# Residuals as identity matmuls in PSUM, norms that read the banks, and ScalarE as writer of the normalized values

## The reference, cut to what matters

```
x = layernorm(x + attention(x))         # attention: projections, conv, state recurrence, gate, @ Wo.T
x_q = where(x > .33, .5, where(x < -.33, -.5, 0))
x = layernorm(x + x_q @ w_rram.T)       # layernorm: (x - mean) / sqrt(var + 1e-5)
```

## Time and profile before

| | us |
|---|---|
| median of 3 runs | 454.32 (451.31 to 454.52) |
| the profiled execution's own time | 453.44 |
| its span, first to last instruction | 451.6 |
| DVE busy | 349.5 (77%) |
| PE busy | 275.5 (61%) |
| ACT busy | 119.8 (27%) |
| mean granted TensorE clock, as a share of full speed | 0.737 |

### The profile page before, as it was taken

How to read it: one execution, slowest core, us unless ns; L and a number is a source line. 1 busy time by engine, 2 the same in 40 slices (tenths; PEclk the granted TensorE clock), 3 DMA queues, 4 the chain that set the end, 5 groups by cost and what they waited for, 6 DMA issues and landing times.

```text
span 451.6 us, 14403 instructions
## 1 busy us (share of the span) xinstructions
PE 275.5 (61%) x6314; PEld 186.1 (41%) x6314; DVE 349.5 (77%) x1154; ACT 119.8 (27%) x245; POOL 56.4 (12%) x62
## 2 busy tenths in 40 slices
PE   3983900498667356876586149795675246786552
PEld 1571600354554135454454127354542235654331
DVE  0755999938699996859799995948899967346986
ACT  0865110046701210355412010357112000133000
POOL 0000440002420200011321000014202000010000
PEclk9955665569768666989676567988686559699785
DMA  8300000000000001000000011000000021000101
GB/s 264 143 0 3 1 0 1 3 3 3 3 4 3 1 4 45 3 3 2 4 4 2 1 48 48 1 3 4 3 3 1 3 93 50 3 3 4 46 1 46
DMA packets 8014, 9.70 MB, mean 21 GB/s; under 512 B 1808, under 2 KB 7056, under 8 KB 7952
## 3 DMA queue, kind: packets, MB, share of 16 engines
q1 hardware_dynamic: 7024, 8.41, 5.6%
q10 hardware_dynamic: 928, 0.38, 0.4%
HBM read 6.70 MB, written 2.10 MB: 19 GB/s over the span
## 4 chain that ended last, share of the span: by engine, by line
DVE 57%; PE 31%; issue 6%; ACT 4%; DMA 1%; DVEq 0%; SPq 0%; ACTq 0%
PE pj L346 7%; PE pc L333 6%; DVE sub_buf L1015 6%; DVE sub_buf L1019 5%; DVE x L1024 4%; PE fr L333 4%; DVE conv_buf L917 3%; PE pg L457 3%; PE fr L572 2%; PE fr L480 2%; PE pj L457 2%; DVE ss L951 2%; DVE stats L1117 1%; DVE r_sb L1065 1%; DVE r_all L905 1%
## 5 line engine op out<-in xcount | busy, mean ns | idle before, releaser
L917 DVE SCALAR_TENSOR_TENSOR conv_buf<-raw,wconv,conv_buf 128x512 f32<-128x512 f32 x72 | 55.5, 776 | 17.0 <-ACT conv_buf L624 15.3
L346 PE MATMUL pj<-xt,wproj 128*128 128x512 f32 x96 | 56.4, 727 | 7.1 <-DMA xt<-x_t 7.1
L333 PE MATMUL fr<-dt_m,chunk_buf 32*32 32x32 f32 x768 | 12.0, 237 | 59.8 <-issue 34.4
L864 POOL TENSOR_TENSOR s_dec<-s_sb,decay 128x192 f32<-128x192 f32 x24 | 14.4, 601 | 238.1 <-DVE s_sb L1074 142.3
L686 ACT ACTIVATE u_sb<-pc 128x192 f32<-128x192 f32 x32 | 10.5, 329 | 111.1 <-PE pc L333 111.0
L333 PE MATMUL pc<-r_sb,t_t 32*32 32x64 f32 x672 | 17.5, 242 | 32.0 <-DVE r_sb L1065 31.3
L333 PEld LDWEIGHTS fr<-dt_m,chunk_buf 32*32 32x32 f32 x768 | 11.2, 151 | 61.4 <-issue 61.4
L346 PEld LDWEIGHTS pj<-xt,wproj 128*128 128x128 f32 x96 | 19.9, 226 | 27.2 <-issue 23.2
L358 PE MATMUL pg<-xt,wproj 128*128 128x512 f32 x48 | 31.0, 778 | 0.0
L333 PEld LDWEIGHTS pc<-r_sb,t_t 32*32 32x32 f32 x672 | 12.3, 119 | 44.2 <-DVE r_sb L1065 40.5
L1019 DVE TENSOR_TENSOR sub_buf<-sub_buf,l 128x12 f32<-128x12 f32 (+14 forms) x120 | 29.7, 286 | 0.0
(11 more groups left out here) (161 smaller groups left out, 580.3 us busy)
## 6 DMA issues: line engine op xcount, KB each, us to landing
xt<-x_t SPq DMA_DIRECT2D x1, 1536.0 KB, 10.2
x_buf<-x SPq DMA_DIRECT2D x3, 512.0 KB, 3.8
out<-hid_buf SPq DMA_DIRECT2D x6, 256.0 KB, 2.2
wproj<-w_proj SPq DMA_DIRECT2D x1, 1024.0 KB, 8.4
xt<-x_t SPq DMA_DIRECT2D x1, 512.0 KB, 5.8
kq<-x SPq DMA_DIRECT2D x1, 512.0 KB, 4.7
out<-v_tok SPq DMA_DIRECT2D x2, 256.0 KB, 2.1
wout<-w_out SPq DMA_DIRECT2D x1, 384.0 KB, 10.5
```

The lines of the kernel that those rows point to most:

```text
L333: mm = pe.matmul(out[rows], stationary[rows], moving[rows], **flags)
L346: mm = pe.matmul(pj[:, j % 2, :], wproj[:, t, j * P:(j + 1) * P], xt[:, t, k * TOK:(k + 1) * TOK], start=(t == 0), stop=(t == KT - 1))
L864: pool.tensor_tensor(s_dec[:, :, :], s_sb[:, :, :], decay[:, :, c:c + 1].to_broadcast([P, G3, DV]), ALU.mult).then_inc(sdec_done, 1)
L917: e = dve.scalar_tensor_tensor(out=conv[:, d, :, :], in0=raw[:, d, :, m:m + T], scalar=wconv[:, j, m:m + 1], in1=conv[:, d, :, :], op0=ALU ...
```

## The change

The residual x is no longer loaded. `project_out` and `end_project_out` first put it into the output bank by matmuls of the transposed x (`xt`, stationary) with an identity matrix (moving), four of 128 columns for each part, and the products accumulate on it. The second part's bank is `fr[:, 1]` in place of `pj[:, 1]`. `feed_forward_products` begins each 256-column piece with an identity matmul of x1, and `end_residual` does this for the last pair.

DVE takes the moments from the banks. It writes `shift` = -mean * reciprocal root, and ACT writes the normalized values by `Identity(scale * in + shift)`: `first_normed` at c = 0, `second_normed` at the end of a turn (behind `u_out` of c = 7 in turn 3). ACT also copies the second sum to `hid` (`feed_forward_out`). `conv_taps(k+1, 1)` moves ahead of `ternary`. In the last pair DVE still writes the normalized values, straight from the banks.

```diff
@@ SP
-            def load_residual(k):
-                after(sp, on_scaled, 1, k, 1)
-                sp.dma_start(res[:, :, :], x_pairs[k, :, :].rearrange(
-                    "(n p) c -> p n c", p=P)).then_inc(ld_res, 16)
...
@@ PE
             def project_out(k, part):
+                if part == 0:
+                    after(pe, gate_done, GATE_TILES, k, GATE_TILES)
+                else:
+                    after(pe, p_done, 2, k + 1, 2)
+                for n in range(2 * part, 2 * part + 2):
+                    for t in range(KT):
+                        cols = slice((n % 2) * HID + t * P, (n % 2) * HID + (t + 1) * P)
+                        pe.matmul(y_bank[part][:, cols], xt[:, t, k * TOK + n * P:k * TOK + (n + 1) * P], ident,
+                                  start=(n % 2 == 0 and t == 0), stop=False, skip_group_check=True)
                 if part == 0:
                     after(pe, og_done, GATE_TILES, k, GATE_TILES)
...
             def feed_forward_products(k, part):
                 if part == 0:
+                    after(pe, x1_done, 1, k, 1)
                     after(pe, xqt_done, 1, k, 1)
...
+                    pe.matmul(fr[:, n // 2, (n % 2) * HID:(n % 2 + 1) * HID], ident, x1[:, n, :],
+                              start=True, stop=False)
...
+            def end_residual(s):
+                pe.wait_ge(end_normed, 2 * (s + 1))
+                for b in range(2):
+                    pe.matmul(fr[:, s, b * HID:(b + 1) * HID], ident, end_x1[:, b, s, :],
+                              start=(b == 0), stop=False, skip_group_check=True)
@@ ACT
+            def normed(k, n, src, dst):
+                return act.activation(dst[:, n, :], src, ACT.Identity, scale=r_n[:, n:n + 1], bias=shift[:, n:n + 1])
+            def first_normed(k):
+                after(act, norm_in, 1, k, 2)
+                for n in range(TT):
+                    e = normed(k, n, y_bank[n // 2][:, (n % 2) * HID:(n % 2 + 1) * HID], x1)
+                e.then_inc(x1_done, 1)
+            def feed_forward_out(k):
+                after(act, hid_moved, 32, k, 32)
+                for n in range(2):
+                    after(act, ffn_mm, n + 1, k, 2)
+                    act.activation(hid[:, 2 * n:2 * n + 2, :].rearrange("p n c -> p (n c)"), fr[:, n, :],
+                                   ACT.Copy).then_inc(ffn_in, 1)
+            def second_normed(k):
+                after(act, norm_in, 2, k, 2)
+                for n in range(TT):
+                    e = normed(k, n, hid[:, n, :], y_out)
...
@@ DVE
-            def attention_sum(k, n):
...
-            def feed_forward_sum(k):
...
+            def shifts():
+                dve.scalar_tensor_tensor(out=shift[:, :], in0=mv[:, :, 0], scalar=-1.0, in1=r_n,
+                                         op0=ALU.mult, op1=ALU.mult).then_inc(norm_in, 1)
...
             def ternary(k):
-                normalize(hid, x1, None)
+                after(dve, x1_done, 1, k, 1)
...
             def end_first_norm(s):
-                dve.wait_ge(end_x, 16)
                 dve.wait_ge(end_y, s + 1)
-                own(dve.tensor_tensor(end_hid[:, :, s, :], y_bank[s].rearrange("p (b c) -> p b c", b=2)
-                                      if s else pg[:, :].rearrange("p (b c) -> p b c", b=2),
-                                      end_x1[:, :, s, :], ALU.add))
-                end_factors(s)
+                if s == 0:
+                    dve.wait_ge(out_done, 2 * (PAIRS - 1))
+                end_factors(end_bank[s])
```

More of the change, by code:

```diff
@@ L200, in program @@
         mv = sb("mv", [P, TT, 2])
+        shift = sb("shift", [P, TT])
         y_out = hid
@@ L309, in store @@
                         "(n p) c -> p n c", p=P), y_out[:, 2 * n:2 * n + 2, :]).then_inc(hid_moved, 16)
[L311 to L317, removed]
             out_last = out_pairs[PAIRS - 1, :, :].rearrange("(b s p) c -> p b s c", b=2, s=2)
-            store(PAIRS - 2)
+            for k in range(PAIRS - 1):
+                store(k)
             for s in range(2):
@@ L486, in end_project_out @@
             def end_project_out(s):
+                if s == 0:
+                    after(pe, gate_done, GATE_TILES, PAIRS - 1, GATE_TILES)
+                for b in range(2):
+                    rows = slice((PAIRS - 1) * TOK + b * T + s * P, (PAIRS - 1) * TOK + b * T + (s + 1) * P)
+                    for t in range(KT):
+                        pe.matmul(end_bank[s][:, b * HID + t * P:b * HID + (t + 1) * P], xt[:, t, rows], ident,
+                                  start=(b == 0 and t == 0), stop=False, skip_group_check=True)
                 pe.wait_ge(end_gated, GATE_TILES * (s + 1))
@@ L602, in _ @@
             end_project_out(1)
+            end_residual(0)
             end_transposes(0)
             end_feed_forward(0)
+            end_residual(1)
             end_transposes(1)
@@ L744, in turn @@
                         ternary_out(k - 1)
+                    if not front and c == NC - 1:
+                        second_normed(k - 1)
                     if front and c == 0:
@@ L751, in turn @@
                         tile_out_of_psum(k + 1, 4)
+                    if tail and c == 2:
+                        feed_forward_out(k - 1)
+                    if front and c == 2:
                         silu(k + 1, 3)
@@ L762, in turn @@
                         tile_out_of_psum(k + 1, 2)
+                    if tail and c == 0:
+                        first_normed(k - 1)
                     if front and c == 2:
@@ L771, in turn @@
                     o_square(k, front)
+                    if tail:
+                        second_normed(k - 1)
                 else:
@@ L1116, in moments @@
                 for n in range(TT):
-                    read = own.counted(dve.bn_stats(stats[:, n, :], src[:, n, :]))
+                    read = own.counted(dve.bn_stats(stats[:, n, :], src(n)))
                 own.until(read)
@@ L1156, in ternary @@
                                          op0=ALU.is_lt, op1=ALU.subtract).then_inc(xq_done, 1)
-            def feed_forward_sum(k):
-                for n in range(2):
-                    after(dve, ffn_mm, n + 1, k, 2)
-                    dve.tensor_tensor(hid[:, 2 * n:2 * n + 2, :].rearrange("p n c -> p (n c)"), fr[:, n, :],
-                                      x1[:, 2 * n:2 * n + 2, :].rearrange("p n c -> p (n c)"),
-                                      ALU.add).then_inc(ffn_in, 1)
             head_v, head_r = ([a[:, UF:U], a[:, 0:UF]] for a in (v_all, r_all))
@@ L1246, in turn @@
                         conv_taps(k + 1, 2)
-                    if tail and c == 2:
-                        feed_forward_sum(k - 1)
                     if front and c == 2:
@@ L1257, in turn @@
                     if tail and c == 3:
-                        moments(hid)
+                        second_moments(k - 1)
                     both = (r_all[:, UF:], v_all[:, UF:], t_all[:, UF:])
@@ L1279, in turn @@
                     next_state(k, c)
+                    if front and c == 0:
+                        conv_taps(k + 1, 1)
                     if tail and c == 0:
                         ternary(k - 1)
-                    if front and c == 0:
-                        conv_taps(k + 1, 1)
                     if front and c == 1:
```

91 lines of the change are left out of this document (39 added, 52 removed).

## The result

The median is 456.89 us (454.07 to 458.74, 20 runs) beside 454.01 (450.78 to 455.34, 20 runs) for the kernel before. The ratio is 1.0061, with an interval of 1.0040 to 1.0082: 2.8 us (1.8 to 3.7) slower, and within the 1% that the prediction calls no change. The profiled execution took 457.1 us, its span is 455.3.

What follows compares the result with a forecast made beforehand. PE was taken to bound the handoff and nearly all of c = 2, DVE c = 0 and the last pair. Terms 3.9 - 0.4 + 0.1 + 2.4 + 2.1 + 0.2 - 2.6 = +5.7 on 453.44 gave 459 us, range 452 to 463.

Steps and rivals of the forecast that it cites:

- Handoff: At project_out, eight x records ahead of part 1 lie unhidden on PE: +1.3 us a turn, +3.9 in all.
- the interpolation by columns: Price of a 128-column record at project_out, set between 0.09 us (12 columns) and 0.24 (256 columns): 0.16 us.
- c = 0: From moments to r_sb, DVE loses four normalizations but waits for ACT: -0.4 us in turns 1 and 2, +0.1 in turn 3.
- ACT's price: For first_normed, 563 ns per 256-column normalization with scale and bias from tiles; four take 1.9 us.
- c = 2: Identity products ahead of the feed-forward pieces lengthen PE's bounding stretch: +2.4 us in turns 1 and 2, +2.1 in turn 3.
- End: End of turn 3 and last pair: normalizations and four sums leave DVE, partly lost to waits; together -2.6 us.
- The square: End of turn 3: ACT's square, queued behind second_normed, ends at 418.6, not 417.2; DVE's reduction still starts 0.5 us sooner.
- the prediction's signs: What would show the forecast right or wrong; for the last pair, right if 2 to 3 us shorter.
- The waits for PE put there: Last pair: DVE loses 0.35 us waiting for the second bank and 0.3 for the last feed-forward.
- 10 ns a read: DVE's extra price for reading a bank in place of SBUF, from two-input instructions at 957 and 948 ns; counted as nothing.
- The clock: Rival: PE stays at 2.4 GHz in part 0 and c = 1; all stretches 450 us, chance 0.12, half 454.5, 0.22.
- ScalarE's queue: Rival: ACT's normalized values cost more or start later, delaying r_sb at c = 0 and turn 3's square; 463 us, chance 0.12.

Runs made afterwards that it cites:

- experiment 1: Changed kernel with the identity products of x for both parts of project_out issued ahead of the wait for the gated values; 453.09 us, ratio 0.9993 to the kernel before.
- experiment 2: Changed kernel without identity products of x1, DVE adding x1 to the banks as before; ratio 0.9884 from three of six times, median of all six 453.78 us.
- experiment 7: Changed kernel with the first normalization back on DVE, reading the banks, and the taps behind the ternary values; 455.42 us, ratio 1.0085 to the kernel before.
- experiment 9: Changed kernel with the last pair's last normalization reading end_x1 in SBUF in place of the bank; 456.03 us, ratio 1.0051 to the kernel before.
- experiment 3: Changed kernel with part 0's x products repeated 6, 4 and 8 times to fill PE's idle time; 449.05 us, ratio 0.9889 to the kernel before.
- experiment 4: Kernel before the change, with 24, 16 and 28 unused identity products ahead of project_out part 0; 444.89 us, ratio 0.9860.
- experiment 6: Changed kernel with unused identity products in PE's wait at c = 1; 451.98 us, ratio 0.9986 to the kernel before.

## Why the prediction was right, and where its sizes were off

The side holds and the time lies inside the range: 459 forecast, 456.89 measured. The movement is half of what was forecast, 2.8 us (1.8 to 3.7) for 5.7, and a range of 452 to 463 would also have held no change at all, so hitting it says little. What was right is which place costs and which gains; the traces bear that out one by one. Their four main terms sum to +4.5 (3.0, -0.4, 4.4 and -2.5), where the prediction has +5.5 for the same four.

- *Handoff.* Forecast +1.3 a turn, found 1.0 us of records in each turn. This is the term with the largest error. The error is the interpolation by columns: 128 columns take 0.125 us a record, not 0.16. Three turns of records are 3.0 us; experiment 1 gives 3.1 by the times, 0.7 of it perhaps by the shorter part 0, which is within its interval.
- *c = 0.* Forecast -0.2 a turn, found -0.23 in turn 1 and as much in turn 2. ACT's price was right to 0.03 us in four (1.9 and 1.93), and so was the idea that the taps hide the wait; 0.98 us of it remain. Turn 3: forecast +0.1, found +0.04 (8.70 to 8.74).
- *c = 2.* Forecast +1.2, +1.2 and +2.1. From r_sb of c = 1 it is +1.4, +1.3 and +1.7, 4.4 in all for 4.5 forecast; experiment 2 puts 4.75 us on these products and the sums that they replace. DVE's idle time was 4.25 us, "some 5" forecast. This is the step that makes the change slower.
- *End.* Forecast -2.6, found -2.5. This agreement is partly luck: it hides two errors. The square was as forecast: gating to the head sums is 0.74 us shorter (2.48 to 1.74), and the forecast's -0.5 counts 0.2 us for the shift ahead of the gating too. One of the four sums of 0.7 us stood ahead of the last pair's first moments. From these to the end of DVE's work it is 1.1 us less (20.98 to 19.90), where the three other sums went. Four pairs of normalizations at 0.26 us more each make up the difference (-2.1 + 1.04). So the pair itself is 1.8 us shorter, and not the "2 to 3" of the prediction's signs. The waits for PE put there, 0.65 us, did not come: DVE's timeline shows no idle time ahead of the moments. In their place each normalization from a bank costs 130 ns more (540 for 410 in the last pair; at c = 0 by experiment 7 533 for 412 by the medians), and that is the sub-step that failed: "10 ns a read" came from a two-input instruction, and a `tensor_scalar` with two scalars from a tile behaves otherwise (experiment 9). The moments do not: two take 0.76 us from the bank in the last pair, and by shape 420 ns from `pg`, 415 from `fr` and 412 from SBUF. The Trainium skill (VectorE: DVE Perf Modes, the section on the TRN2 errata) states for VectorE a fixed term of 120 cycles with a PSUM source and 58 with an SBUF source; from this we estimate 65 ns more for a read of a bank, at the 0.96 GHz that the page gives. Neither kind of instruction here agrees with one such term: 120 to 130 ns more for the one, and 2 to 9 for the others.
- *The clock.* Given 0.12 and 0.22. In the stretches that it named it did not happen in the changed kernel: part 0 ran at 5.49, 4.17 and 5.27 us, 14.9 in all where it was 14.7 before, and c = 1 at 5.5 us twice. It did happen where the prediction had not looked, in the last pair, by the change's own products. PE's timeline of the kernel before, then of the changed one, which also answers to the feed-forward of the earlier trace rows:

```profile
418.04 4.39 PE L491 MATMUL pg<-wout,conv_buf 128*128 128x256 f32 x12 [2.08 <-DVE conv_buf L1200]
```

```profile
424.31 2.86 PE L500 MATMUL pg<-wout,conv_buf 128*128 128x256 f32 x12 [0.99 <-DVE conv_buf L1232]
442.83 1.13 PE L509 MATMUL fr<-kq,cst 128*128 128x256 f32 x4 [1.79 <-DVE kq L1252]
445.11 1.48 PE L525 MATMUL fr<-wsplit,tok_buf 128*128 128x256 bf16 x12 [0.69 <-ACT tok_buf L765]
```

The output product of the first half went from 4.39 to 2.86 us and the last feed-forward from 2.74 to 1.48. The first is 2.86 in all eleven executions with the change in them and 4.4 to 4.5 in the three without, the second 1.48 or 1.49 in ten of eleven and 2.74 in all three. It gave no time, since DVE bounds the last pair; the feed-forward would have been ready 0.4 us early at half clock too. The price given for the three stretches of part 0 was about right, 6.0 us. When they were filled the time fell by 7.8 us (experiment 3, where part 0 accounts for 6.5 and c = 1 of turn 2 ran at 3.8 us too) and by 6.4 (experiment 4). For c = 1 the price was too low: 1.1 us a turn forecast, 1.65 and 1.68 found in turns 1 and 2 (experiment 6). The 4.58 us of the earlier trace rows were not all at 1.2 GHz, as the prediction has them: the granted clock was 0.50 up to 175.0 and 0.67 behind.
- *ScalarE's queue* did not bind: 567 to 579 ns an instruction from a bank, for 563 forecast, where it needed 0.2 us more. From SBUF it took 586.

What stays open: the segments of the profiled pair sum to +5.3, the executions timed differ by 2.8 (at most 3.7). Of the segments, 4.5 are the four terms, 0.3 is part 0's own length, and the rest lies behind the s_sb of c = 2. Since c = 1 and part 0 take different lengths in the same code, one execution of each can't settle a difference of 2 us. That the times lie below the segments was not traced to a place.

## What to carry to other kernels

Work taken from an engine with the highest busy share is worth what the waits at that place say: here DVE gave up 14.8 us, and where PE was the bound it all came back as DVE's waiting. Here new work for PE cost nothing where PE waits and its full length where one product follows another, so put each piece ahead of the wait, not behind it. Look first for long products at half the granted clock behind an idle stretch: cheap products that nobody uses, placed in that stretch, gave 6 to 8 us of 454, more than the whole change moved.

## What was not expected of the hardware

- A normalization (128x256, both scalars from a tile) takes 407 to 412 ns from SBUF and 533 to 540 from a bank on DVE (medians by place); moments take 409 to 418 and 416 to 420.
- ACT takes 567 to 579 ns from a bank and 586 from SBUF for 128x256 with scale and bias from tiles.
- A float32 record of 128 columns takes 0.125 us at full clock (eight in 1.0 us), one of 256 columns 0.23.
- The same `project` behind 2.62 us of idle PE took 3.22 us, and 1.94 behind 0.84; but in another execution 1.94 behind 2.63.
